# Setup phase: one weight group is turned while the group before it is mixed, with two sets of turned weights

## The chip, the cores and the metric

The kernel runs on one core of one Trainium2 chip. The metric is the device time of one launch in microseconds; three runs of the kernel before gave 2410.3 us as median (2406.4 to 2411.33).

TensorE (PE in the profile) multiplies and transposes into PSUM, ScalarE (ACT) and VectorE (DVE) read PSUM and write SBUF, GpSimd (POOL) works in SBUF only, SyncE (SP) issues the DMAs. The engines run their own instruction streams and meet at semaphores only.

## What is computed

The reference is a small network over 4 x 512 tokens of width 512: an attention with random features (L0), a layer that routes each token to one of 64 tiles and adds a spline of 8 of its dimensions, a differential attention (L1), and a gated feed-forward whose three weight matrices are turned by Walsh-Hadamard transforms. For this change two parts matter:

```
# L1 feed-forward: x and weights pass through a Hadamard transform (fwht) with signs SU
W_up, W_gate: 2048 x 512      W_down: 512 x 2048
# L0 feed-forward, routing of each token (xf: normalised tokens)
input_sigs = sign(xf)
best_cluster = argmax(input_sigs @ cluster_sigs.T)
tile_idx = argmax(where(in_cluster, input_sigs @ tile_sigs.T, -inf))
x_slice = xf at the 8 dimensions of that tile; tile_min, tile_max over all tokens of a tile
```

The kernel folds the transforms into the weights once, in a setup phase, and does the routing of the L0 layer for the first use of it in the same phase. Everything else comes after that phase.

## The kernel before

All weights are kept as two float16 parts, high and low: ScalarE writes the high part of a PSUM block, VectorE the difference between the block and its high part.

The setup phase (`setup_sync`, `setup_pool`, `setup_tensor`, `setup_scalar`, `setup_vector`) first turns three groups of L0 attention weights (`first`, lines 797 and 932 on), normalises the tokens, and then runs a loop of four chunks i. A chunk takes three weight groups: two of W_up or W_gate (g = 0, 1) and 128 rows of W_down (g = 2), and routes 512 tokens.

- `turned(i, g)` is four tiles r. TensorE transposes 4 blocks of 128x128 float32 into PSUM bank 0 or 1 (`turn_rows`, line 719), ScalarE writes the high part (line 810), VectorE the low part (line 951), into the one buffer pair `wt_hi`, `wt_lo`. Tile r waits for the low part of tile r-2, which frees its bank.
- `mixed(i, g)` is four blocks kc, and waits for all four tiles of the group. For g = 0, 1 a block is 8 matmuls of 512 columns (line 762), for g = 2 it is 2 (lines 765, 766); into bank 2 or 3, then high part (lines 817, 822) and low part (lines 959, 965). Block kc waits for the low part of block kc-2.
- The W_down rows are scaled by ScalarE (`scale_down`, line 827) and go through four butterfly stages on GpSimd (lines 696, 697) before they are turned.
- The routing of a chunk is a chain over three engines: ScalarE normalises four token tiles (line 845); for each of four feature blocks c TensorE turns it (`route_turn`, line 459) and ScalarE adds gamma and beta and takes the sign (lines 512, 515); TensorE scores the tiles (`route_key`, lines 470, 472), VectorE picks the best (lines 530, 531), TensorE and ScalarE turn the choice (`route_hot`, lines 481, 522), TensorE spreads it as a mask and VectorE multiplies it in (lines 492, 540), TensorE gathers the eight dimensions (`route_slice`, line 502), VectorE keeps the extremes (`route_ends`, lines 548 to 558).

Each engine has these steps in a fixed order written out in its setup function; TensorE's is turned 0, mixed 0, four route turns, turned 1, key, mixed 1, hot, turned 2, masks, two blocks of mixed 2, slice, the other two blocks. SyncE loads the weight groups in order into two halves of `nat`, and stores each finished W_down chunk (`store_down`) to DRAM.

After the loop `minmax_tensor` and `minmax_vector` (lines 597 to 607) reduce the extremes, and the next phase starts.

Of the kernel before, what the change touches and what calls it, by code (L numbers as in the profile page):

```python
# [28 lines left out]
NCH = NTOK // CH  # L29
# [248 lines left out]
def place(k, nc, ctx):  # L278
# [35 lines left out]
    k.wd_nat, a = v.at(a, [P, 4, INTER], F32)  # L314
# [4 lines left out]
    k.wt_hi, a = v.at(a, [P, KC, HID], F16)  # L319
    k.wt_lo, a = v.at(a, [P, KC, HID], F16)  # L320
# [309 lines left out]
def setup_sync(k, sp):  # L630
# [54 lines left out]
def setup_pool(k, e):  # L685
    s = k.s
    e.wait_ge(s["all_chain"], 5)
    for o in range(4):
        e.wait_ge(s["wd_scaled"], o + 1)
        bufs = [k.wd_nat[:, o, :], k.wd_tmp]  # L690
# [17 lines left out]
def tile_base(i, g):  # L708

    return 4 * (W0_GROUPS + 3 * i + g)  # L710


def setup_tensor(k, pe):
# [24 lines left out]
    def turned(i, g):  # L738
        tile = tile_base(i, g)
        if g < 2:  # L740
            buf = (W0_GROUPS + g) % 2
            pe.wait_ge(s[f"nat_in{buf}"], 32 * ((W0_GROUPS + g) // 2 + 1 + i))
        else:
            pe.wait_ge(s["wd_mixed"], i + 1)
        for r in range(4):
            pe.wait_ge(s["wt_lo"], tile + r - 1)
            if g < 2:
                native(buf, r, UP_BANK[r % 2])
            else:
                turn_rows(lambda c, r=r: k.wd_nat[:, i, (4 * r + c) * P:(4 * r + c + 1) * P], UP_BANK[r % 2])  # L750

    def mixed(i, g, blocks):
        pe.wait_ge(s["wt_lo"], tile_base(i, g) + 4)
        for kc in blocks:
            pe.wait_ge(s["had_lo"], 4 * (3 * i + g) + kc + 3)
            bank = HAD_BANK[kc % 2]
            if g < 2:
                n = 0
                for jc in range(KC):
                    sign = k.had16n if bin(kc & jc).count("1") & 1 else k.had16  # L760
                    for part in (k.wt_hi, k.wt_lo):
                        ins = pe.matmul(k.ps[:, bank, :], sign, part[:, jc, :], start=(n == 0), stop=(n == 7))  # L762
                        n += 1
            else:
                pe.matmul(k.ps[:, bank, :], k.had16, k.wdt_hi[:, 4 * kc:4 * kc + 4, :], start=True, stop=False)
                ins = pe.matmul(k.ps[:, bank, :], k.had16, k.wdt_lo[:, 4 * kc:4 * kc + 4, :], start=False, stop=True)
            ins.then_inc(s["had_done"], 1)

    pe.wait_ge(s["ss_chain"], 5)
    for i in range(NCH):  # L770
        turned(i, 0)
        mixed(i, 0, range(KC))
        for c in range(KC):
            route_turn_tensor(k, pe, i, 1, c, ROUTE_BANK)
        turned(i, 1)
        route_key_tensor(k, pe, i, 1, KEY_BANK)
        mixed(i, 1, range(KC))
        route_hot_tensor(k, pe, i, 1, ROUTE_BANK[0])
        turned(i, 2)
        for c in range(KC):  # L780
            route_mask_tensor(k, pe, i, 1, c, ROUTE_BANK)
        mixed(i, 2, (0, 1))
        route_slice_tensor(k, pe, i, 1, KEY_BANK)
        mixed(i, 2, (2, 3))
    pe.wait_ge(s["had_lo"], 4 + 4 * 3 * NCH)


def setup_scalar(k, e):
# [15 lines left out]
    def turned(i, g):  # L804
        tile = tile_base(i, g)
        for r in range(4):
            e.wait_ge(s["nat_turned"], tile + r + 1)
            src = k.ps[:, UP_BANK[r % 2], :].rearrange("p (c m) -> p c m", c=KC)
            dst = k.wt_hi[:, :, r * P:(r + 1) * P] if g < 2 else k.wdt_hi[:, 4 * r:4 * r + 4, :]
            e.activation(dst, src, ACT.Copy, scale=W_SCALE).then_inc(s["wt_hi"], 1)  # L810

    def mixed(i, g):
        for kc in range(KC):
            e.wait_ge(s["had_done"], 4 * (3 * i + g) + kc + 1)
            src = k.ps[:, HAD_BANK[kc % 2], :]
            if g < 2:
                e.activation(ug_block(k, 2 * i + g, 0, kc), src.rearrange("p (f m) -> p f m", m=P), ACT.Copy,
                             scale=k.su_ug[:, kc:kc + 1]).then_inc(s["had_hi"], 1)
            else:
                if kc == 0 and i:  # L820
                    e.wait_ge(s["wdo_out"], 32 * i)
                e.activation(k.wdo_hi[:, 4 * kc:4 * kc + 4, :], src.rearrange("p (c m) -> p c m", c=4), ACT.Copy,
                             scale=float(INTER) ** -0.5).then_inc(s["had_hi"], 1)

    def scale_down(o):
        e.wait_ge(s[f"wd_in{o}"], 16)
        e.activation(k.wd_nat[:, o, :], k.wd_nat[:, o, :], ACT.Copy, scale=k.wscale_dp[:, o:o + 1])\
            .then_inc(s["wd_scaled"], 1)
# [12 lines left out]
    for i in range(NCH):  # L841
        turned(i, 0)
        for u in range(TPC):
            t = i * TPC + u
            ins = e.activation(k.y[:, u, :], k.x[:, t, :], ACT.Identity, bias=k.wide[6][:, t:t + 1],
                               scale=k.wide[5][:, t:t + 1])
        ins.then_inc(s["z_scaled"], 1)
        mixed(i, 0)
        for c in range(KC):
            route_sign_scalar(k, e, i, 1, c, ROUTE_BANK)  # L850
        turned(i, 1)
        if i + 1 < NCH:
            scale_down(i + 1)
        mixed(i, 1)
        route_hot_scalar(k, e, i, 1, ROUTE_BANK[0])
        turned(i, 2)
        mixed(i, 2)
# [43 lines left out]
def setup_vector(k, V):  # L901
# [43 lines left out]
    def turned(i, g):  # L945
        for r in range(4):
            e.wait_ge(s["wt_hi"], tile_base(i, g) + r + 1)
            src = k.ps[:, UP_BANK[r % 2], :].rearrange("p (c m) -> p c m", c=KC)
            hi, lo = [w[:, :, r * P:(r + 1) * P] if g < 2 else x[:, 4 * r:4 * r + 4, :]
                      for w, x in ((k.wt_hi, k.wdt_hi), (k.wt_lo, k.wdt_lo))]  # L950
            e.scalar_tensor_tensor(out=lo, in0=src, scalar=W_SCALE, in1=hi, op0=ALU.mult, op1=ALU.subtract)\  # L951
                .then_inc(s["wt_lo"], 1)

    def mixed(i, g, blocks):
        for kc in blocks:
            e.wait_ge(s["had_hi"], 4 * (3 * i + g) + kc + 1)
            src = k.ps[:, HAD_BANK[kc % 2], :]
            if g < 2:
                e.scalar_tensor_tensor(out=ug_block(k, 2 * i + g, 1, kc), in0=src.rearrange("p (f m) -> p f m", m=P),
                                       scalar=k.su_ug[:, kc:kc + 1], in1=ug_block(k, 2 * i + g, 0, kc),  # L960
                                       op0=ALU.mult, op1=ALU.subtract).then_inc(s["had_lo"], 1)
            else:
                if kc == 0 and i:
                    e.wait_ge(s["wdo_out"], 32 * i)
                e.scalar_tensor_tensor(out=k.wdo_lo[:, 4 * kc:4 * kc + 4, :], in0=src.rearrange("p (c m) -> p c m", c=4),
                                       scalar=float(INTER) ** -0.5, in1=k.wdo_hi[:, 4 * kc:4 * kc + 4, :],
                                       op0=ALU.mult, op1=ALU.subtract).then_inc(s["had_lo"], 1)
                e.wait_ge(s["had_lo"], 4 + 4 * (3 * i + g) + kc + 1)
                e.sem_inc(s["wdo_lo"], 1)
# [7 lines left out]
    for i in range(NCH):  # L977
        turned(i, 0)
        mixed(i, 0, range(KC))
        turned(i, 1)  # L980
        route_choice_vector(k, V, i, 1, KEY_BANK)
        mixed(i, 1, range(KC))
        turned(i, 2)
        for c in range(KC):
            route_pick_vector(k, V, i, 1, c, ROUTE_BANK)
        mixed(i, 2, (0, 1))
        mixed(i, 2, (2, 3))
        route_ends_vector(k, V, i, 1, KEY_BANK)
# [1671 lines left out]
def bass_macaron(nc, d):  # L2660
    with ExitStack() as ctx:
# [7 lines left out]
        k.wdt_hi = k.wt_hi.rearrange("p c (b m) -> p (c b) m", m=P)  # L2669
        k.wdt_lo = k.wt_lo.rearrange("p c (b m) -> p (c b) m", m=P)  # L2670
# [158 lines left out]
```

## Time and profile before

| what | value |
|---|---|
| median of three runs | 2410.3 us |
| profiled execution: its own time, its span | 2407.47 us, 2405.7 us |
| PE, DVE, ACT, POOL busy over the span | 2087.0, 1228.1, 749.2, 221.2 us |
| setup loop with its last reduction | 38.3 to 254.4 us of the span |
| PE busy in it, granted clock | 166.09 of 216.10 us, 0.75 |
| DVE, ACT busy in it | 90.94 us, 97.82 us |

The span is the stretch between the first and the last instruction of the profiled execution. The granted clock is the share of TensorE's full clock that the chip allowed: 1.00 is 2.4 GHz and 0.50 is 1.2 GHz. A row of a timeline merges instructions of one kind that follow each other: start, duration, engine, line, operation, output and input, count, and in brackets the idle time before it with what ended it.

### The profile page before, as it was taken

How to read it: one execution, taken by the hardware profiler on the slowest of the kernel's cores; microseconds unless marked ns; L12 is line 12 of the kernel's file. 1: busy time of each engine (PE TensorE's matmuls, PEld its weight loads, DVE VectorE, ACT ScalarE, POOL GpSimd, SP SyncE). 2: the span in 40 equal slices, each digit the busy share in tenths (PEclk: the TensorE clock that was granted, in tenths of full speed). 3: DMA queues.
4: the chain of work that ended last, by engine and by line, in shares of the span. 5: the costliest groups of instructions: out<-in, count | busy, mean ns of one | idle time of the engine just before them, and what ended most of it. 6: DMA issues, size and time to landing. Idle time of an engine off the chain costs nothing. (4 is left out here: it accounts for less than half of the span.)

```text
span 2405.7 us, 29600 instructions
## 1 busy us (share of the span) xinstructions
PE 2087.0 (87%) x12078; PEld 996.0 (41%) x12078; DVE 1228.1 (51%) x2281; ACT 749.2 (31%) x1163; POOL 221.2 (9%) x164
## 2 busy tenths in 40 slices
PE   4777486878877479999999999989998999999998
PEld 3444333333435234444444444434443444444443
DVE  5444445657554445555557445653566356623332
ACT  4444123333242122223234322442235123511211
POOL 3341021211110000000100010001000000000000
PEclk7777577988785589999999999999999999999999
DMA  6211402021112212222111111111111111222322
GB/s 247 88 53 18 164 10 48 22 37 28 31 49 58 93 55 94 97 97 75 41 43 62 36 62 54 53 45 53 53 54 53 53 39 34 78 88 98 114 92 74
DMA packets 90978, 158.75 MB, mean 66 GB/s; under 512 B 44182, under 2 KB 55772, under 8 KB 86108
## 3 DMA queue, kind: packets, MB, share of 16 engines
q1 hardware_dynamic: 90844, 156.86, 20.3%
q8 instruction: 96, 1.57, 0.3%
q14 instruction: 38, 0.31, 0.0%
HBM read 128.52 MB, written 18.87 MB: 61 GB/s over the span
## 5 line engine op out<-in xcount | busy, mean ns | idle before, releaser
L1130 PE MATMUL ps<-arena 128*128 128x512 f16 (+1 forms) x4512 | 1019.1, 381 | 19.8 <-DVE arena L1893 12.9
L1130 PEld LDWEIGHTS ps<-arena 128*128 128x128 f16 x4512 | 437.2, 99 | 541.4 <-issue 48.5
L1838 PE MATMUL ps<-arena 128*128 128x512 f16 x1536 | 348.9, 383 | 29.5 <-DVE arena L1884 16.3
L1838 PEld LDWEIGHTS ps<-arena 128*128 128x128 f16 x1536 | 147.4, 98 | 207.3 <-issue 29.2
L1860 ACT ACTIVATE arena<-ps,arena 128x512 f32<-128x512 f32 x128 | 87.6, 684 | 362.3 <-PE ps L1130 362.0
L1893 DVE SCALAR_TENSOR_TENSOR arena<-arena,ps 128x512 f32<-128x512 f32 x128 | 87.9, 686 | 210.1 <-ACT arena L1860 209.5
L2447 ACT ACTIVATE arena<-ps 128x1024 f32<-128x1024 f32 (+3 forms) x128 | 90.1, 704 | 253.7 <-PE ps L2356 253.7
L2552 DVE CAST arena<-arena 128x1024 f16<-128x1024 f32 (+3 forms) x128 | 66.6, 520 | 149.7 <-ACT arena L2447 147.7
L2518 DVE TENSOR_REDUCE arena<-ps 128x2 f32<-128x256 f32 (+3 forms) x128 | 99.6, 819 | 65.1 <-PE ps L2300 65.1
L1902 DVE SCALAR_TENSOR_TENSOR arena<-ps,arena 128x512 f32<-128x512 f32 x128 | 95.8, 748 | 39.3 <-PE ps L1130 39.1
L1921 DVE SCALAR_TENSOR_TENSOR arena<-ps,arena 128x512 f32<-128x512 f32 x64 | 44.0, 687 | 139.6 <-PE ps L1838 139.4
L2554 DVE TENSOR_TENSOR arena<-arena 128x1024 f16<-128x1024 f32 (+3 forms) x128 | 111.4, 870 | 4.4
L1529 DVE TENSOR_TENSOR arena<-ps,arena 128x256 f32<-128x256 f32 x128 | 47.8, 418 | 100.9 <-PE ps L1214 100.9
L2498 POOL TENSOR_TENSOR arena<-arena 128x512 f16<-128x512 f32 x32 | 37.1, 1159 | 656.7 <-ACT arena L2425 656.7
L1884 DVE TENSOR_TENSOR arena<-arena 128x512 f16<-128x512 f32 x128 | 91.7, 716 | 4.0 <-ACT arena L1852 4.0
L1755 PE MATMUL ps<-arena 128*128 128x128 f32 x192 | 33.6, 335 | 67.0 <-ACT arena L1970 67.0
L1852 ACT ACTIVATE arena<-arena 128x512 f16<-128x512 f32 x128 | 79.7, 622 | 17.5 <-DVE arena L1902 17.5
L719 PE MATMUL ps<-arena 128*128 128x128 f32 x240 | 43.8, 341 | 43.0 <-DVE arena L951 30.2
L762 PE MATMUL ps<-arena 128*128 128x512 f16 x256 | 72.0, 451 | 5.7 <-DVE arena L951 5.7
L2354 PE MATMUL ps<-arena 32*128 32x512 f16 (+3 forms) x768 | 72.9, 293 | 0.0
L2502 POOL TENSOR_TENSOR arena<-arena 128x512 f32<-128x512 f32 x16 | 18.6, 1161 | 582.0 <-DVE arena L2565 582.0
L2422 ACT ACTIVATE arena<-ps 128x512 f32<-128x512 f32 x32 | 19.1, 597 | 166.7 <-PE ps L1130 166.7
(267 smaller groups left out, 2466.5 us busy)
## 6 DMA issues: line engine op xcount, KB each, us to landing
arena<-wug_dram SPq DMA_DIRECT2D x128, 512.0 KB, 3.3
arena<-wd_hi_dram SPq DMA_DIRECT2D x16, 1024.0 KB, 5.0
arena<-wd_lo_dram SPq DMA_DIRECT2D x16, 1024.0 KB, 7.3
arena<-arena SPq DMA_DIRECT2D x144, 64.0 KB, 2.1
wug_dram<-arena SPq DMA_DIRECT2D x4, 2048.0 KB, 16.5
arena<-_attn_hidden_states_dram SPq DMA_DIRECT2D x4, 1024.0 KB, 11.8
arena<-in_L_ffn_W_up_dram SPq DMA_DIRECT2D x8, 512.0 KB, 4.4
arena<-in_L_ffn_W_down_dram SPq DMA_DIRECT2D x4, 1024.0 KB, 8.0
```

The lines of the kernel that those rows point to most:

```text
L762: ins = pe.matmul(k.ps[:, bank, :], sign, part[:, jc, :], start=(n == 0), stop=(n == 7))
L1130: ins = pe.matmul(out, left[a](c), right[b](c), start=(at == 0), stop=(at == 3 * n - 1))
L1838: ins = pe.matmul(k.ps[:, bank, :], act[x][:, slot, cols], wd[y][:, f, :], start=(f == 0 and m == 0), stop=(f == 7 and m == 2))
L1852: e.activation(k.act_hi[:, g % ACT_SLOTS, :], k.prod[:, g % 2, :], ACT.Copy).then_inc(s["f_hi"], 1)
L1860: e.activation(k.th[:, g % 2, :], k.ps[:, GATE_BANK, :], ACT.Tanh, scale=k.wscale[:, FB + a:FB + a + 1])\
L1884: e.tensor_tensor(k.act_lo[:, g % ACT_SLOTS, :], k.prod[:, g % 2, :], k.act_hi[:, g % ACT_SLOTS, :], ALU.subtract)\
L1893: e.scalar_tensor_tensor(out=th, in0=th, scalar=1.0, in1=k.ps[:, GATE_BANK, :], op0=ALU.add, op1=ALU.mult)\
L1902: e.scalar_tensor_tensor(out=k.prod[:, g % 2, :], in0=k.ps[:, UP_HALF_BANK, :], scalar=k.wscale[:, a:a + 1], in1=th, op0=ALU.mult, op1=ALU ...
L2354: pe.matmul(k.ps[:, bank, queries], x[rows, 4 + b, keys], y[rows, b, queries], start=False, stop=False)
L2447: e.activation(k.p32[:, t % 2, :, queries], k.ps[:, 0:2, queries], ACT.Exp, scale=SCORE).then_inc(s["c_exp"], 1)
L2518: e.tensor_reduce(k.mx[:, u, 4 * b + 2 * j:4 * b + 2 * j + 2], k.ps[:, bank:bank + 2, 0:(u + 1) * P], AXX, ALU.max).then_inc(s["c_max"], 1)
L2554: e.tensor_tensor(k.p_lo[:, t % 2, :, queries], k.p32[:, t % 2, :, queries], k.p_hi[:, t % 2, :, queries], ALU.subtract).then_inc(s["c_p_l ...
```

## The change

The loop over chunks and groups becomes one loop over n = 0 to 12 (n = 3i + g) and over steps r = 0 to 3. Step (n, r) is tile r of group n and then block r of group n-1. The turned weights get a second buffer pair (side n % 2). To make room `wd_nat` keeps three rows of chunks instead of four; the fourth load of W_down goes into the first slot again, behind a wait on TensorE's transposes of group 2, and is issued one place later in SyncE's order. The routing is cut into its steps and each stands at a fixed place (`ROUTE_AT`: groups after 3i, step). `scale_down(i + 1)` moves from behind `turned(i, 1)` to behind the normalising of chunk i. All instructions on the four compute engines are the same in kind and number.

```diff
-    k.wd_nat, a = v.at(a, [P, 4, INTER], F32)
+    k.wd_nat, a = v.at(a, [P, 3, INTER], F32)
...
-    k.wt_hi, a = v.at(a, [P, KC, HID], F16)
-    k.wt_lo, a = v.at(a, [P, KC, HID], F16)
+    k.wt = []
+    for side in range(2):
+        hi, a = v.at(a, [P, KC, HID], F16)
+        lo, a = v.at(a, [P, KC, HID], F16)
+        k.wt.append((hi, lo))
...
-        if g < 4:
-            sp.dma_start(k.wd_nat[:, g, :], d["L1_ffn_W_down"][g * P:(g + 1) * P, :]).then_inc(s[f"wd_in{g}"], 16)
+        o = g if g < 3 else 3
+        if g < 3 or g == 4:
+            if o == 3:
+                sp.wait_ge(s["nat_turned"], 4 * (W0_GROUPS + 3))
+            sp.dma_start(k.wd_nat[:, o % 3, :], d["L1_ffn_W_down"][o * P:(o + 1) * P, :]).then_inc(s[f"wd_in{o}"], 16)
...
+ROUTE_AT = {"stats": (0, 1), "turn": ((0, 3), (1, 0), (1, 1), (1, 2)), "sign": ((1, 0), (1, 1), (1, 2), (1, 3)),
+            "key": (2, 0), "hot": (2, 1), "mask": ((2, 2), (2, 2), (2, 3), (2, 3)), "slice": (3, 0), "ends": (3, 1)}
...
+def route_now(n, r, what, c=None):
+    at = ROUTE_AT[what] if c is None else ROUTE_AT[what][c]
+    i = n // 3 if at[0] < 3 else n // 3 - 1
+    return i if 0 <= i < NCH and (n - 3 * i, r) == at else None
...
# setup_tensor
+    def turned(n, r):
...
+        pe.wait_ge(s["wt_lo"], tile_base(n) + r - 1)
...
+    def mixed(n, kc):
+        if kc == 0:
+            pe.wait_ge(s["wt_lo"], tile_base(n) + 4)
+        pe.wait_ge(s["had_lo"], 4 * n + kc + 3)
...
-    for i in range(NCH):
-        turned(i, 0)
-        mixed(i, 0, range(KC))
-        for c in range(KC):
-            route_turn_tensor(k, pe, i, 1, c, ROUTE_BANK)
-        turned(i, 1)
-        route_key_tensor(k, pe, i, 1, KEY_BANK)
-        mixed(i, 1, range(KC))
-        route_hot_tensor(k, pe, i, 1, ROUTE_BANK[0])
-        turned(i, 2)
-        for c in range(KC):
-            route_mask_tensor(k, pe, i, 1, c, ROUTE_BANK)
-        mixed(i, 2, (0, 1))
-        route_slice_tensor(k, pe, i, 1, KEY_BANK)
-        mixed(i, 2, (2, 3))
+    for n in range(GROUPS + 1):
         for r in range(4):
+            if n < GROUPS:
+                turned(n, r)
+            if n:
+                mixed(n - 1, r)
+            for c in range(KC):
+                i = route_now(n, r, "turn", c)
+                if i is not None:
+                    route_turn_tensor(k, pe, i, 1, c, ROUTE_BANK)
...
# setup_scalar: per step turned, mixed, then
+            i = route_now(n, r, "stats")
+            if i is not None:
+                for t in range(i * TPC, (i + 1) * TPC):
+                    ins = e.activation(k.y[:, t % TPC, :], k.x[:, t, :], ACT.Identity, bias=k.wide[6][:, t:t + 1],
+                                       scale=k.wide[5][:, t:t + 1])
+                ins.then_inc(s["z_scaled"], 1)
+                if i + 1 < NCH:
+                    scale_down(i + 1)
...
# then route_sign and route_hot; setup_vector: per step turned, mixed, then choice, picks, ends
```

## Rows read from the trace of the kernel before

**Rows 1.** The page: the granted clock in 40 slices of the span.

```profile
PEclk7777577988785589999999999999999999999999
```

**Rows 2.** Busy time by stretch: stretch, length, then PE, PEld, DVE, ACT, POOL, clock, DMA.

```profile
140.80:195.20 54.40, 42.55 (x197) 25.08 (x196) 22.77 (x38) 24.98 (x38) 18.62 (x8) 0.75 0.19 59
38.30:254.40 216.10, 166.09 (x776) 97.67 (x776) 90.94 (x152) 97.82 (x152) 74.56 (x32) 0.75 0.19 56
```

**Rows 3.** Groups of instructions, 38 to 254 us: busy and mean, idle before.

```profile
L762 PE MATMUL ps<-arena 128*128 128x512 f16 x256 | 72.0, 451 | 5.7 <-DVE arena L951 5.7
L719 PE MATMUL ps<-arena 128*128 128x128 f32 x184 | 32.2, 325 | 30.2 <-DVE arena L951 30.2
...
L817 ACT ACTIVATE arena<-ps,arena 128x512 f16<-128x512 f32 x32 | 22.0, 687 | 46.5 <-PE ps L762 46.5
```

**Rows 4.** Timeline of PE, from the first chunk's slice into the second chunk.

```profile
78.16 6.92 PE L502 MATMUL ps<-arena 128*128 128x8 f32 x32
...
86.58 1.87 PE L719 MATMUL ps<-arena 128*128 128x128 f32 x8
91.98 1.97 PE L719 MATMUL ps<-arena 128*128 128x128 f32 x8 [3.53 <-DVE arena L951]
95.37 8.63 PE L762 MATMUL ps<-arena 128*128 128x512 f16 x32 [1.41 <-DVE arena L951]
...
107.27 1.04 PE L719 MATMUL ps<-arena 128*128 128x128 f32 x8
...
112.77 0.23 PE L470 MATMUL ps<-arena 1*128 1x64 f16 x1
...
114.60 5.57 PE L762 MATMUL ps<-arena 128*128 128x512 f16 x15
```

**Rows 5.** Busy time and granted clock of the later part of that mixing.

```profile
98.80:103.80 5.00, 5.00 (x25) 2.11 (x23) 2.25 (x3) 2.06 (x3) 0.00 (x0) 1.00 0.00 1
```

**Rows 6.** Timeline of ACT.

```profile
36.37 2.00 ACT L827 ACTIVATE arena<-arena 128x2048 f32<-128x2048 f32 x1 [3.43 <-DVE arena L898]
...
94.48 2.92 ACT L845 ACTIVATE arena<-arena 128x512 f32<-128x512 f32 x4
...
106.76 0.63 ACT L515 ACTIVATE arena<-arena 128x512 f16<-128x512 f32 x1
107.30 0.76 ACT L512 ACTIVATE arena<-ps,arena 128x512 f32<-128x512 f32 x1
...
109.96 1.06 ACT L810 ACTIVATE arena<-ps 128x512 f16<-128x512 f32 x2
```

**Rows 7.** Timeline of DVE.

```profile
88.30 0.30 DVE L548 TENSOR_SCALAR arena<-arena 128x256 f32<-128x256 f16 x1
...
91.24 1.29 DVE L951 SCALAR_TENSOR_TENSOR arena<-ps,arena 128x512 f16<-128x512 f32 x2
...
103.03 0.75 DVE L959 SCALAR_TENSOR_TENSOR arena<-ps,arena 128x512 f16<-128x512 f32 x1 [0.99 <-ACT arena L817]
...
128.84 1.28 DVE L540 TENSOR_TENSOR arena<-ps,arena 128x512 f32<-128x512 f32 x2
```

**Rows 8.** Busy time and granted clock of three other stretches.

```profile
12.00:18.00 6.00, 5.92 (x33) 5.68 (x32) 4.42 (x11) 3.76 (x7) 0.00 (x0) 1.00 1.05 393
...
130.80:140.80 10.00, 10.00 (x41) 8.07 (x41) 2.16 (x4) 1.79 (x3) 3.56 (x2) 0.50 0.00 0
...
143.00:144.00 1.00, 0.00 (x0) 0.00 (x0) 0.93 (x4) 0.35 (x1) 0.00 (x0) 1.00 0.28 72
```

**Rows 9.** Timeline of POOL: the last butterfly of the first chunk.

```profile
55.05 2.37 POOL L697 TENSOR_TENSOR arena<-arena 128x1024 f32<-128x1024 f32 x1
```

**Rows 10.** Timeline around the loop's end.

```profile
251.88 1.26 SPq L664 DMA_DIRECT2D wd_lo_dram<-arena  x1
...
254.00 0.29 DVE L558 TENSOR_TENSOR arena<-arena 128x128 f32<-128x128 f32 x1
...
260.70 0.55 DVE L2767 COPY arena<-arena 24x768 f32<-24x768 f32 x1 [4.51 <-DMA arena<-in_L_attn_bo_dram]
```

More of the change, by code:

```diff
@@ L736, in setup_tensor @@
             native(g % 2, r, r)
-    def turned(i, g):
-        tile = tile_base(i, g)
+    def turned(n, r):
+        i, g = n // 3, n % 3
+        if r == 0:
+            if g < 2:
+                group = W0_GROUPS + 2 * i + g
+                pe.wait_ge(s[f"nat_in{group % 2}"], 32 * (group // 2 + 1))
+            else:
+                pe.wait_ge(s["wd_mixed"], i + 1)
+        pe.wait_ge(s["wt_lo"], tile_base(n) + r - 1)
         if g < 2:
-            buf = (W0_GROUPS + g) % 2
-            pe.wait_ge(s[f"nat_in{buf}"], 32 * ((W0_GROUPS + g) // 2 + 1 + i))
-        else:
-            pe.wait_ge(s["wd_mixed"], i + 1)
-        for r in range(4):
[L746 to L767, printed above, removed]
@@ L785, in setup_tensor @@
-    pe.wait_ge(s["had_lo"], 4 + 4 * 3 * NCH)
+            native((W0_GROUPS + g) % 2, r, UP_BANK[r % 2])
+        else:
+            turn_rows(lambda c: k.wd_nat[:, i % 3, (4 * r + c) * P:(4 * r + c + 1) * P], UP_BANK[r % 2])
+    def mixed(n, kc):
+        if kc == 0:
+            pe.wait_ge(s["wt_lo"], tile_base(n) + 4)
+        pe.wait_ge(s["had_lo"], 4 * n + kc + 3)
+        out = k.ps[:, HAD_BANK[kc % 2], :]
+        if n % 3 < 2:
+            m = 0
+            for jc in range(KC):
+                sign = k.had16n if bin(kc & jc).count("1") & 1 else k.had16
+                for part in range(2):
+                    ins = pe.matmul(out, sign, k.wt[n % 2][part][:, jc, :], start=(m == 0), stop=(m == 7))
+                    m += 1
+        else:
+            for part in range(2):
+                ins = pe.matmul(out, k.had16, k.wdt[n % 2][part][:, 4 * kc:4 * kc + 4, :], start=(part == 0),
+                                stop=(part == 1))
+        ins.then_inc(s["had_done"], 1)
@@ new lines, in setup_tensor @@
+    pe.wait_ge(s["ss_chain"], 5)
+    for n in range(GROUPS + 1):
+        for r in range(4):
+            if n < GROUPS:
[6 more added lines that the diff above has]
+                    route_turn_tensor(k, pe, i, 1, c, ROUTE_BANK)
+            i = route_now(n, r, "key")
+            if i is not None:
+                route_key_tensor(k, pe, i, 1, KEY_BANK)
+            i = route_now(n, r, "hot")
+            if i is not None:
+                route_hot_tensor(k, pe, i, 1, ROUTE_BANK[0])
+            for c in range(KC):
+                i = route_now(n, r, "mask", c)
+                if i is not None:
+                    route_mask_tensor(k, pe, i, 1, c, ROUTE_BANK)
+            i = route_now(n, r, "slice")
+            if i is not None:
+                route_slice_tensor(k, pe, i, 1, KEY_BANK)
@@ L788, in setup_scalar @@
+    pe.wait_ge(s["had_lo"], 4 + 4 * GROUPS)
 def setup_scalar(k, e):
@@ L840, in setup_scalar @@
     scale_down(0)
[L841 to L857, printed above, removed]
+    for n in range(GROUPS + 1):
+        for r in range(4):
+            if n < GROUPS:
+                turned(n, r)
+            if n:
+                mixed(n - 1, r)
+            i = route_now(n, r, "stats")
+            if i is not None:
+                for t in range(i * TPC, (i + 1) * TPC):
[4 more added lines that the diff above has]
+                    scale_down(i + 1)
+            for c in range(KC):
+                i = route_now(n, r, "sign", c)
+                if i is not None:
+                    route_sign_scalar(k, e, i, 1, c, ROUTE_BANK)
+            i = route_now(n, r, "hot")
+            if i is not None:
+                route_hot_scalar(k, e, i, 1, ROUTE_BANK[0])
 def setup_stats_vector(k, V):
@@ L943, in first @@
                 .then_inc(s["wt_lo"], 1)
[L945 to L969, printed above, removed]
+    def turned(n, r):
+        e.wait_ge(s["wt_hi"], tile_base(n) + r + 1)
+        e.scalar_tensor_tensor(out=turned_block(k, n, r, 1),
+                               in0=k.ps[:, UP_BANK[r % 2], :].rearrange("p (c m) -> p c m", c=KC), scalar=W_SCALE,
+                               in1=turned_block(k, n, r, 0), op0=ALU.mult, op1=ALU.subtract).then_inc(s["wt_lo"], 1)
@@ L976, in setup_vector @@
     setup_norm_vector(k, V)
[L977 to L988, printed above, removed]
+    for n in range(GROUPS + 1):
+        for r in range(4):
+            if n < GROUPS:
+                turned(n, r)
+            if n:
+                mixed(n - 1, r)
+            i = route_now(n, r, "key")
+            if i is not None:
+                route_choice_vector(k, V, i, 1, KEY_BANK)
+            for c in range(KC):
+                i = route_now(n, r, "mask", c)
+                if i is not None:
+                    route_pick_vector(k, V, i, 1, c, ROUTE_BANK)
+            i = route_now(n, r, "ends")
+            if i is not None:
+                route_ends_vector(k, V, i, 1, KEY_BANK)
 def apply_tensor(k, pe, i, n):
```

67 lines of the change are left out of this document (41 added, 26 removed).

## The prediction

> **What bounds the kernel now.** The page comes first: the granted clock stands at 0.7 to 0.8 in four of the first five slices and is low in the next ones too, against 0.9 later [rows 1]; the change touches only the setup loop, which lies in the first slices. So next the busy time by stretch. From 38.3 to 254.4 us PE is busy 166.09 of 216.10 us, ACT 97.82, DVE 90.94, at a clock of 0.75; a chunk takes 54.40 us with PE busy 42.55 [rows 2]. Two things are wrong in the loop: 50 us in which PE waits, and matmuls at half clock. The groups of instructions name the wait: transposes sit idle 30.2 us until VectorE has written a low part (L951), the first matmul of a mixing another 5.7 us, and neither waits for a DMA [rows 3]. The timeline of one chunk shows how [rows 4]: eight transposes at 86.58, idle, eight more at 91.98, idle, and the mixing at 95.37: 8.8 us for 3.8 us of work, and PE has nothing else in its order to do. Of the mixing, 32 matmuls in 8.63 us, the first 3.4 us are slow; from 98.8 on the clock stands at 1.00 [rows 5]. So a block of eight matmuls costs 3.4 us at 1.2 GHz and (8.63 - 3.4) / 3 = 1.74 us at 2.4 GHz.
>
> What follows the loop is released by its end (the last extremes, then a bias load issued after them) [rows 10], so what the loop saves comes off the span nearly one for one.
>
> **The change, part by part.** Durations used. A tile of four transposes costs PE 0.43 us at full clock and 0.9 at half (eight in 1.04, with the pipeline's tail, and in 1.87) [rows 4]; a W_down block a quarter of a wide one. ACT: 0.53 for a tile (two in 1.06), 0.76 + 0.63 for a sign step, 2.92 for normalising, 2.00 for scaling W_down [rows 6], 0.69 for a block [rows 3]. DVE: 0.65 a tile (two in 1.29), 0.75 a block, 0.64 a pick (two in 1.28), 2.9 for the extremes (88.30 to the next group at 91.24) [rows 7].
>
> *Two sets of turned weights, tile and block in turn.* This removes the wait at the start of a mixing and fills the idle time between tiles with blocks. The waits are the old ones in new places. Tile r waits for the low part of tile r-2, and behind it in PE's queue stand the block of the same step and the route step; two steps are at least 4.3 us of PE work in the wide groups, and the hand-over PE to ACT to DVE and back costs about 2.5 us (a tile's 0.9 at half clock, ACT 0.6, DVE 0.7 and the gaps), so it is met there. A block waits for the block two before; from PE's end to DVE's end is 0.25 + 0.72 + 0.75 = 1.7 us (gap, ACT, DVE), and a block and two tiles lie between. Now a chunk, laid out by all three engines, in three parts.
>
> Part A, from the last block of group 3i-1 (time 0) to the first block of group 3i. DVE has the low part of that block and two picks behind it: 1.7 + 1.3 = 3.0 us, so the slice starts at 3.2. The slice (L502) took 6.92 us [rows 4], and the slices here run at half clock (0.50 in the stretch that holds the second one) [rows 8]. At full clock it has no row. From above it is bounded by 6.9 us; from below by half, 3.4, as transposes with weights of the same shape halve. It would start with the clock up and lose it on the way: I take 5.1 us, the middle, and keep both ends. Then PE does tile 1 and block 1, ACT evicts them (2.1 us after the slice), and now ACT is the queue: normalising and scaling stand ahead of tile 2, 2.92 + 2.00, until 7.1 us; tiles 2 and 3 and the block between them take it to 8.9, DVE to 9.9. The first block of group 3i starts 10.0 us after the slice. Part A is 3.2 + 5.1 + 10.0 = 18.3 us. The scaling comes here from a place where ACT had time: 2.0 us of these are a cost of the move.
>
> Part B, the four blocks of group 3i beside the tiles of 3i+1 and the sign steps. The first block runs at half clock after PE idled in part A: 3.4 us. The other three steps are bounded by ACT, 0.53 + 0.69 + 0.76 + 0.63 = 2.6 us and a gap, 2.75 each (PE has 0.43 + 1.74 + 0.43 = 2.6): 8.2 us. Then 1.4 us until the fourth tile, evicted behind the third sign step, is there. 13.0 us.
>
> Part C, the blocks of group 3i+1: PE sets the pace, as ACT (1.2 us) and DVE (1.4 us, 2.7 with picks) have little more per step. Block 1.7, key 1.9 (112.77 to 114.60, at half clock) [rows 4], three steps of 0.43 + 1.74 = 6.5, hot and two masks 0.8 (estimated by their columns). 10.9 us.
>
> A chunk is 18.3 + 13.0 + 10.9 = 42.2 us instead of 54.4.
>
> *Start.* In group 0 ACT has scaling (until 38.3), two tiles, normalising, scaling again, two tiles: 38.3 + 1.06 + 2.92 + 2.00 + 1.06 = 45.4, DVE 46.2, first block at 46.4. Group 2 is turned from about 58 us on, and POOL ends the W_down rows it needs at 57.4 [rows 9]: just in time. Parts B and C end at 46.4 + 13.0 + 10.9 = 70.3.
>
> *End.* Three more chunks: 70.3 + 126.6 = 196.9. Then 3.2 for the picks, 5.1 for the slice, 5.2 for block 1 through ACT and DVE (2.3) and the extremes (2.9): 210.4, where the trace has 254.3 (254.00 + 0.29) [rows 10]: 43.9 us less.
>
> *Tail.* VectorE now has two blocks behind the extremes, 1.5 us, and SyncE stores the last W_down chunk behind them (the second half alone took 1.26 us to issue) before it may load the biases; now the wait from the extremes to the end of that load is 6.4 us (254.3 to 260.70) [rows 10]. I charge 4 us, between 1.5 (the blocks alone) and 6 (the load lands late behind the store).
>
> *At no cost.* The fourth W_down load goes into a slot free since group 2 and is needed three groups (some 40 us) later. Loads of the next groups are issued when a half of `nat` is turned and needed two groups later; the waits of stores stand ahead of some of them in SyncE's order, with more than a group to spare. If that cover were gone, PE rows would wait for a DMA.
>
> Sum: 43.9 - 4 = 40 us. The profiled execution took 2407.47 us around a span of 2405.7, 2.8 us below the median; against the median the forecast is 2410.3 - 40 = 2370 us.
>
> **The clock, weighed.** That parts B and C run at full clock is what the forecast needs. The rows for it: PE is at 0.50 up to 140.8, and after two small blocks and eight transposes that follow the slice it stands at 1.00 at 143 us, with PE already idle again [rows 8]. A step of part B has 1.74 us of wide matmuls in 2.75, more than that.
>
> The Trainium skill ("TensorE: Matmul & The Clock Gate", Part 4, PE-mode transpose) says that transposes do not count as busy for the clock gate the way matmuls do. By it, a loop that mixes transposes into matmuls dilutes the work that counts, which speaks for the first rival below. The trace half agrees: from 12 to 18 us PE did 32 transposes and nothing else and stayed at 1.00 [rows 8].
>
> **Rivals.**
> 1. *The alternation keeps the clock at 1.2 GHz* (slower). 28 blocks that I put at 1.74 us would take 3.4, 47 us, and tiles and route steps some 15 us more: 40 - 62 = -22, 2432 us. It turns the sign from about 24 slow blocks of 28. For it: no stretch of this trace thins out matmuls in this way. Against it: the rows just named. 4%.
> 2. *The waits only move.* Each engine serves two streams in one order, so a late eviction holds both. If each of seven steps of B and C in four chunks pays half a hand-over again, 1.2 us, 34 us are lost: 2404 us. For it: ACT is nearly full in part B. Against it: every wait reaches two steps back. 12%, for a gain between 5 and 20 us.
> 3. *More than forecast.* Slice at full clock (4 x 1.7 = 7 us), and the clock back before part B's first block (4 x 1.7 = 7 us): 54 us, 2356 us. 16%.
> 4. *SyncE's order holds a load, or POOL is late*: the wait appears on a DMA or on L697 and eats the gain, 2405 to 2415 us. 3%.
>
> The forecast's own case has 65%.
>
> **How the numbers follow.** Ends: 7 us each way for the slice, 7 each way for when the clock rises, 2 for the tail, and up to 0.3 us for hand-overs left out in each of 52 steps, 15 us, one way only. Best 2354, worst 2401; I give 2352 to 2395, which leaves out rivals 1 and 4 and part of 2. A change under 0.2% (5 us) could not be told from none. Faster by more holds the forecast, rival 3 and most of 2: 0.92; same 0.03; slower 0.05.
>
> **What would show it.** The idle time ahead of L719 and L762 (36 us together) falls to about 15, nearly all of it in part A. The granted clock of the loop rises from 0.75 to 0.85 or more. After each slice PE idles while ACT runs L845 and L827. The last row of the extremes moves from 254.0 to about 210, and what follows keeps its length but for 4 us. It would be wrong if L762's blocks stay 3.4 us long, if ACT idles ahead of L512 in part B, or if PE waits for a DMA or for POOL.

## The result and the profile after

The kernel after takes 2364.3 us as median of four runs (2363.24 to 2367.23), the kernel before, in the same comparison, 2410.2 (2406.4 to 2411.33): a ratio of 0.9817, interval 0.9801 to 0.9832. Forecast were 2370 us, 40 us less; 45.9 us came off. The profiled execution took 2363.24 us around a span of 2361.5, 44.2 us less than the span before. (The 1.7 us between 45.9 and 44.2 are scatter: the profiled execution before lies 2.7 us under its median, the one after 1.0 us under its own.)

The granted clock of the page, the busy time of the loop (columns as in [rows 2]), and the groups of PE instructions in it (as [rows 3]; L790 was L762, L747 was L719, L505 was L502):

```profile
PEclk7886769797966599999999999999999999999999
```
```profile
38.30:205.80 167.50, 144.53 (x776) 90.16 (x776) 89.05 (x150) 95.67 (x152) 74.67 (x32) 0.83 0.24 72
```
```profile
L790 PE MATMUL ps<-arena 128*128 128x512 f16 x256 | 65.6, 402 | 2.8 <-DVE arena L985 2.8
L747 PE MATMUL ps<-arena 128*128 128x128 f32 x184 | 33.7, 315 | 11.5 <-DVE arena L985 11.5
L505 PE MATMUL ps<-arena 128*128 128x8 f32 x128 | 23.2, 323 | 5.3 <-DVE arena L543 5.3
```

The loop with its last extremes takes 167.5 us instead of 216.1 [rows 2]. The wait ahead of transposes and wide blocks is 14.3 us (11.5 + 2.8) instead of 35.9 [rows 3], the clock 0.83 instead of 0.75. PE's busy time falls by 21.6 us (166.09 to 144.53) with the same instructions, and its idle time by 27.0 (50.0 to 23.0): the two add up to the loop's gain. VectorE's count falls by two because its last two blocks now stand behind the extremes. Nothing in the loop waits for a DMA or for the butterflies.

PE from the first slice to the second chunk's blocks (beside [rows 4]):

```profile
72.87 5.24 PE L505 MATMUL ps<-arena 128*128 128x8 f32 x32 [1.21 <-DVE arena L543]
...
77.96 1.09 PE L747 MATMUL ps<-arena 128*128 128x128 f32 x4
78.85 1.06 PE L794 MATMUL ps<-arena 128*128 128x512 f16 x2
...
83.41 0.66 PE L462 MATMUL ps<-arena 128*128 128x128 f32 x4 [0.84 <-ACT arena L884]
86.67 1.09 PE L747 MATMUL ps<-arena 128*128 128x128 f32 x4 [2.61 <-DVE arena L985]
88.02 3.60 PE L790 MATMUL ps<-arena 128*128 128x512 f16 x8 [0.26 <-DVE arena L985]
91.41 0.85 PE L462 MATMUL ps<-arena 128*128 128x128 f32 x4
92.09 0.60 PE L747 MATMUL ps<-arena 128*128 128x128 f32 x4
92.53 1.89 PE L790 MATMUL ps<-arena 128*128 128x512 f16 x8
...
95.13 1.89 PE L790 MATMUL ps<-arena 128*128 128x512 f16 x8
```

Read the durations of equal blocks: 3.60 us at 88.02 and 1.89 at 92.53 (each with the tail that the model adds to a duration), and from 92.53 on one block starts every 2.60 us. And ACT in the same stretch, which is why PE idles 2.61 us: normalising (L884) and scaling (L861) stand ahead of the eviction of the tile (L843).

```profile
80.44 2.92 ACT L884 ACTIVATE arena<-arena 128x512 f32<-128x512 f32 x4
83.26 1.99 ACT L861 ACTIVATE arena<-arena 128x2048 f32<-128x2048 f32 x1
85.15 0.58 ACT L843 ACTIVATE arena<-ps 128x512 f16<-128x512 f32 x1
```

The loop's end, DVE and then SyncE's queue, which stores W_down (L667) and then loads the biases (L687, L688) (beside [rows 10]):

```profile
205.54 0.29 DVE L561 TENSOR_TENSOR arena<-arena 128x128 f32<-128x128 f32 x1
...
216.72 0.55 DVE L2805 COPY arena<-arena 24x768 f32<-24x768 f32 x1 [7.56 <-DMA arena<-in_L_attn_bo_dram]
```
```profile
208.04 1.24 SPq L667 DMA_DIRECT2D wd_lo_dram<-arena  x1
209.32 2.99 SPq L687 DMA_DIRECT2D arena<-in_L_attn_bv_dram  x1
212.36 0.58 SPq L688 DMA_DIRECT2D arena<-in_L_attn_bo_dram  x1
```

The extremes end 48.5 us earlier (205.83 against 254.29), and the copy behind them starts 10.9 us later than that, instead of 6.4: 4.5 us are given back. At the copy 44.0 of the span's 44.2 us are in.

### The profile page after: what moved, and what is told of

It reads as the page before. It is cut to its first block and busy times, and to the rows that moved or that the text cites. A ratio compares the mean times of both kernels' runs of the same rounds, so it can differ in the third digit from the quotient of the medians.

```text
span 2361.5 us, 29596 instructions
## 1 busy us (share of the span) xinstructions
PE 2062.1 (87%) x12078; PEld 987.3 (42%) x12078; DVE 1227.2 (52%) x2281; ACT 746.9 (32%) x1163; POOL 220.9 (9%) x164
## 5 line engine op out<-in xcount | busy, mean ns | idle before, releaser
L1169 PEld LDWEIGHTS ps<-arena 128*128 128x128 f16 x4512 | 436.4, 99 | 542.8 <-issue 48.5
L1877 PE MATMUL ps<-arena 128*128 128x512 f16 x1536 | 349.0, 383 | 29.5 <-DVE arena L1923 16.3
L790 PE MATMUL ps<-arena 128*128 128x512 f16 x256 | 65.6, 402 | 2.8 <-DVE arena L985 2.8
L747 PE MATMUL ps<-arena 128*128 128x128 f32 x240 | 45.3, 334 | 24.3 <-DVE arena L985 11.5
```

Source lines behind the costliest of these rows:

```text
L1169: ins = pe.matmul(out, left[a](c), right[b](c), start=(at == 0), stop=(at == 3 * n - 1))
L1877: ins = pe.matmul(k.ps[:, bank, :], act[x][:, slot, cols], wd[y][:, f, :], start=(f == 0 and m == 0), stop=(f == 7 and m == 2))
```

## The experiments

Times are medians; "gain" is the difference to the kernel before in the same comparison, whose median was 2406.5 us for the first four kernels, 2408.0 for the next four and 2409.3 for the last four (three comparisons, each on another chip). The last three columns come from one profiled execution each: where the last row of the extremes starts, where the copy behind the loop starts, and how much of the span is left from there.

| kernel | us | gain | ratio, interval | last extremes start | copy starts | span left |
|---|---|---|---|---|---|---|
| the kernel before | | | | 254.00 | 260.70 | 2145.0 |
| the change | 2364.3 | 45.9 | 0.9817 (0.9801 to 0.9832) | 205.54 | 216.72 | 2144.8 |
| the change again | 2362.9 | 43.6 | 0.9824 (0.9808 to 0.9840) | 205.80 | 217.81 | 2143.2 |
| e1_whole_groups | 2375.2 | 31.2 | 0.9862 (0.9838 to 0.9885) | 213.00 | 224.24 | 2148.6 |
| e2_routing_lumps | 2363.7 | 42.8 | 0.9818 (0.9802 to 0.9835) | 205.79 | 217.13 | 2146.4 |
| e7_short_slice | 2341.7 | 64.8 | 0.9733 (0.9717 to 0.9749) | 185.28 | 196.39 | 2140.5 |
| e3_scale_late | 2371.3 | 36.7 | 0.9850 (0.9837 to 0.9864) | 214.06 | 225.41 | 2143.1 |
| e4_slice_late | 2351.7 | 56.2 | 0.9768 (0.9755 to 0.9782) | 190.45 | 201.45 | 2145.1 |
| e5_bias_apart | 2354.5 | 53.5 | 0.9784 (0.9771 to 0.9798) | 204.94 | 208.59 | 2139.4 |
| e8_warm | 2355.7 | 52.3 | 0.9777 (0.9764 to 0.9791) | 199.93 | 211.68 | 2144.6 |
| e9_late_apart | 2342.0 | 67.3 | 0.9714 (0.9699 to 0.9729) | 190.51 | 194.16 | 2145.5 |
| e10_late_apart_warm | 2334.9 | 74.4 | 0.9688 (0.9675 to 0.9701) | 191.82 | 195.47 | 2145.3 |
| e11_scale_ahead | 2360.9 | 48.4 | 0.9789 (0.9775 to 0.9804) | 201.56 | 213.23 | 2149.1 |
| e12_all | 2332.0 | 77.3 | 0.9682 (0.9667 to 0.9697) | 183.80 | 187.45 | 2140.1 |

Only the bias wait of four kernels (e5, e9, e10, e12) was changed behind the copy, and yet the span left varies from 2139.4 to 2149.1 us. So a difference of a few us between two medians is laid to the loop only where the loop's end in the traces moves by as much.

**The change again** gives the scale for what a repeat moves.

> The changed kernel once more, on the same chip as the three that follow, to compare them with. Every theory: 2363 to 2367 us, the last row of the extremes at about 206 us of the span.

2362.9 us, 0.1 us under the range, and the same loop's end to 0.3 us. Within the loop the repeat isn't the same: the last chunk's first wide block takes 3.23 us, where the change had 1.90, and the last slice 5.38 instead of 6.66.

**Two sets, but whole groups.** All four tiles, then all four blocks, in all three instruction streams; the routing and the scaling keep the places that the change gave them:

```diff
         for r in range(4):
             if n < GROUPS:
                 turned(n, r)
+        for r in range(4):
             if n:
                 mixed(n - 1, r)
```

> The second set of turned weights stays, the alternation goes: on every engine the four tiles of group n come together, then the four blocks of group n-1. Theory (tile and block in turn fill the waits): tiles 2 and 3 of each group wait again for the low parts of tiles 0 and 1, which stand behind the last block and sign step on ScalarE; about 1.2 us in parts with a free ScalarE, 3.5 us beside the signs, about 25 to 30 us in all 13 groups: 2388 to 2396 us, most of it as idle time ahead of the transposes. Rival (the second set alone brings the gain, since the mixing no longer waits for its own tiles): 2364 to 2370 us.

```profile
L790 PE MATMUL ps<-arena 128*128 128x512 f16 x256 | 65.5, 401 | 0.0
L747 PE MATMUL ps<-arena 128*128 128x128 f32 x184 | 32.4, 323 | 23.4 <-DVE arena L987 23.4
L505 PE MATMUL ps<-arena 128*128 128x8 f32 x128 | 15.7, 263 | 1.4 <-DVE arena L543 1.4
```

It fell between the two. By the medians everything but the alternation is worth 31 of the 43 to 46 us, and the alternation adds 12. The traces make the second share smaller: at the copy this kernel is 36.5 us ahead of the kernel before and 6.4 behind the change again, and the other 5.4 us between the two profiled executions arise behind the copy, where the kernels are the same. With a group turned ahead the blocks never wait (0.0); without the alternation transposes wait 23.4 us instead of 11.5, and part of that comes back at the slices, three of which start without idle time and take 3.63 us each (15.7 us for four instead of 23.2). What the second set does without the routing's and the scaling's new places no run shows.

**Routing in lumps.** All feature turns, signs and masks of a chunk at one place each:

```diff
-"turn": ((0, 3), (1, 0), (1, 1), (1, 2)), "sign": ((1, 0), (1, 1), (1, 2), (1, 3)),
+"turn": ((1, 0),) * 4, "sign": ((1, 0),) * 4,
-"mask": ((2, 2), (2, 2), (2, 3), (2, 3))
+"mask": ((2, 2),) * 4
```

> The alternation stays, the routing is taken in lumps: all four feature turns and signs after block 0 of part B, all four masks and picks at step 2 of part C. Theory (TensorE's order blocks behind a chain that goes to and fro): about 2 us per chunk at the signs, since ScalarE is the limit there anyway, and 3 us at the masks: 20 us over four chunks, 2380 to 2388 us. Rival (where the routing stands does not matter, only that blocks and tiles alternate): 2364 to 2368 us.

The theory fell, the rival's number held: the same time. But the trace shows a trade, and not the absence of effect that the rival named:

```profile
L747 PE MATMUL ps<-arena 128*128 128x128 f32 x184 | 32.1, 304 | 20.0 <-DVE arena L985 19.6
L505 PE MATMUL ps<-arena 128*128 128x8 f32 x128 | 14.5, 253 | 0.0
```

Transposes wait 8.5 us more and the mask products 7.6 us where they had waited for nothing, but the picks are through long before the slice, which waits for nothing (5.3 us less) and runs at full clock throughout: 14.5 us for four instead of 23.2. So the stepwise routing as such is worth nothing here; what it gains in the steps it loses at the slice.

**A quarter of the slice.** In the setup phase each slice does 4 of its 16 products, which the trace shows as 8 of 32 matmuls (so the eight dimensions are incomplete):

```diff
         for c in range(KC):
+            if one and c:
+                continue
```

> Leaves out 12 of the 16 matmuls of each slice in the setup loop, so the extremes are taken over a part of the features only. Theory (the slice lies whole on the path, and while it runs the granted clock falls, which makes the next wide block slow): the slice falls from 5.1 to 6.7 us to about 1.3, 4 x 4.3 = 17 us, and up to 3 x 1.7 = 5 us more where the clock then stays up: 2342 to 2348 us. Rival (part A is bounded by ScalarE's queue and VectorE's extremes, the slice is half covered): 2352 to 2358 us.

The time is the theory's within 0.3 us, 21 us against the change again, but only its first half is borne out. The four slices take 4.5 us instead of 23.2, 18.7 us less, and the loop ends 20.3 us earlier than in the change: the slice lies on the path with its whole length. The blocks behind it are no faster on the whole: the first blocks of the three chunks take 2.86, 3.44 and 3.03 us, where the change had 3.60, 3.50 and 1.90.

**The scaling moved behind the one-hot of the same chunk**, out of the stretch behind the slice:

```diff
                 ins.then_inc(s["z_scaled"], 1)
-                if i + 1 < NCH:
-                    scale_down(i + 1)
...
                 route_hot_scalar(k, e, i, 1, ROUTE_BANK[0])
+                if i + 1 < NCH:
+                    scale_down(i + 1)
```

> The scaling of the next W_down rows moves from behind the normalising in part A to behind the choice in part C, where ScalarE has time. Theory (its 2.0 us stand in the queue ahead of tile 2 and so ahead of the next wide block; where the extremes run too, VectorE is free 1.5 us earlier only): 2.0 + 3 x 1.5 = 5 to 6 us less than the changed kernel, 2357 to 2359 us. Rival (part A is bounded by VectorE's extremes or by GpSimd, which now gets its rows later): no gain, 2363 us or more.

It got slower than the change, by 7 to 9 us. The rival's "2363 us or more" covers the time, but it spoke of a missing gain; neither named a loss. DVE's extremes, and POOL's butterflies at the same time, which the scaling releases:

```profile
79.92 1.16 DVE L551 TENSOR_SCALAR arena<-arena 128x256 f32<-128x256 f16 x1
81.00 0.18 DVE L554 TENSOR_REDUCE arena<-ps 128x4 f32<-128x32 f32 x1
...
81.42 1.97 DVE L557 TENSOR_SCALAR arena<-arena 128x4 f32<-128x4 f32 x1
83.42 2.79 DVE L559 TENSOR_TENSOR arena<-arena 128x512 f32<-128x512 f32 x1
86.24 1.02 DVE L560 TENSOR_REDUCE arena<-arena 128x128 f32<-128x512 f32 x1
```
```profile
78.57 2.36 POOL L703 TENSOR_TENSOR arena<-arena 128x1024 f32<-128x1024 f32 x1
81.01 2.35 POOL L702 TENSOR_TENSOR arena<-arena 128x1024 f32<-128x1024 f32 x1
83.32 2.34 POOL L703 TENSOR_TENSOR arena<-arena 128x1024 f32<-128x1024 f32 x1
```

In the change L551, L557 and L559 take 0.29, 0.16 and 0.69 us. Here the first two end when POOL's instruction does, at 81.08 against 80.93 and 83.39 against 83.36; the third ends at 86.21, POOL's end at 85.66 and 0.55 more. The operations beside them that read PSUM keep their 0.18 us. The extremes start 1.5 us earlier and end 3.2 us later (87.59 against 84.35), and behind them wait the low parts: PE idles 5.89 us ahead of the tile instead of 2.61. In the next two chunks it idles 3.95 and 4.31 us instead of 2.61 and 0.94; together that is 8.0 us more, and the loop ends 8.5 later. In the change POOL begins its butterflies at 85.39, 1.0 us after the extremes, and misses them.

The Trainium skill has this ("SBUF — State Buffer", Who interferes with whom): VectorE and GpSimd share a port pair as an exclusive lock, held for a whole instruction; a VectorE instruction with two SBUF inputs, or in a two-port mode, takes part, and one with at most one SBUF input outside these modes does not. This trace agrees for L559, which has two SBUF inputs, and for the operations that read PSUM. L551 and L557 have one and were held too, to within 0.15 us of POOL's end; by the page they would have to be in a two-port mode, which no run here shows. I had not weighed this beforehand.

**The slice a step later**, behind block 1 instead of ahead of it; ACT waits for it before it overwrites the tokens:

```diff
-"slice": (3, 0)
+"slice": (3, 1)
...
+                if i:
+                    e.wait_ge(s["r_slice"], i)
```

> The slice stands one step later, behind tile 1 and block 1, and the normalising waits for the slice itself. Theory (TensorE idles 1.2 us ahead of the slice, tile 1 and block 1 fit there, and after the slice ScalarE starts the normalising at once): 2.6 us per chunk on three chunks and 2.3 us at the end, 10 us less than the changed kernel, 2352 to 2356 us. Rival (the slice's end is not what ScalarE's queue starts from; or the clock is lost as before and tile and block only change places): at most 3 us, 2360 us or more.

```profile
71.83 3.74 PE L505 MATMUL ps<-arena 128*128 128x8 f32 x32 [0.34 <-DVE arena L543]
```

The sum is as the theory had it (0.3 us under its range), the parts are not. Tile 1 and block 1 fill the wait for the picks, and ACT starts the normalising when the slice ends; but three of four slices also keep the clock and take 3.74 us, which the theory had not priced. Of the 15.1 us by which the loop ends earlier than in the change, the slices are 5.8, and 1.0 is there ahead of the first slice already (by the medians the gain is 10 to 13 us; the profiled execution is the fastest of its five). The last slice took 6.19, with 0.59 us of idle time ahead of it.

**The bias loads on another semaphore**, waited for only where the biases are used (TensorE's wait falls to 128 too):

```diff
-    sp.dma_start(k.bv, ...).then_inc(s["b_in"], 16)
-    sp.dma_start(k.bo, ...).then_inc(s["b_in"], 16)
+    sp.dma_start(k.bv, ...).then_inc(s["const_in"], 16)
+    sp.dma_start(k.bo, ...).then_inc(s["const_in"], 16)
...
-        dve.wait_ge(s["b_in"], 160)
+        dve.wait_ge(s["b_in"], 128)
...
+            dve.wait_ge(s["const_in"], 48)
```

> The two bias loads at the loop's end count on a semaphore of their own, which VectorE waits for only 27 us later, where they are long there; nothing else changes. Theory (VectorE's wait of 7.6 us for the last bias load is on the path, 4.5 us of the alternation's gain were lost in that tail): 7 us less than the changed kernel, 2355 to 2358 us. Rival (the next phase waits for other loads or for the store of W_down anyway): within 2 us of the changed kernel, 2361 to 2365 us.

```profile
204.94 0.29 DVE L561 TENSOR_TENSOR arena<-arena 128x128 f32<-128x128 f32 x1
...
208.59 0.55 DVE L2805 COPY arena<-arena 24x768 f32<-24x768 f32 x1
```

As the theory had it, and half a us more: the loop is as in the change (its end 0.6 us earlier), the copy waits for nothing and starts 8.1 us earlier.

**Added products** in an unused bank around the first feature turn of chunks 1 to 3:

```diff
+                    if c == 0 and i:
+                        warm(4)
                     route_turn_tensor(k, pe, i, 1, c, ROUTE_BANK)
+                    if c == 0 and i:
+                        warm(8)
```

> Adds 12 matmuls of 512 columns per chunk into an unused bank, 4 ahead of the first feature turn and 8 behind it, where TensorE idles in part A. Theory (the wide blocks at the start of part B run at half clock because TensorE idled before them): first blocks of 1.7 instead of 3.4 us in two or three chunks, 3 to 5 us less, 2358 to 2361 us. Rival (the clock falls during the slice and comes back by the blocks alone, or the added matmuls run at half clock and delay the next tile): 0 to 5 us more, 2363 to 2369 us.

```profile
83.02 1.89 PE L800 MATMUL ps<-arena 128*128 128x512 f16 x8
85.80 0.63 PE L747 MATMUL ps<-arena 128*128 128x128 f32 x4 [0.88 <-DVE arena L993]
87.14 1.90 PE L790 MATMUL ps<-arena 128*128 128x512 f16 x8 [0.72 <-DVE arena L993]
```

By the medians it is more than expected, 6 to 9 us. In the trace the extremes end 5.6 us earlier than in the change, and 1.3 of these are there at the first slice, ahead of any added product; the other 4.3 lie in the theory's 3 to 5. Filling the idle time brings the first block of part B to 1.90 us in all three chunks (3.60, 3.50 and 1.90 in the change), and in chunk 1 the tile ahead of it to 0.63 where it took 1.09.

**Combinations, and the scaling once more.** e9 is e4 and e5, e10 adds the products of e8.

> The slice one step later (as e4_slice_late) together with the two bias loads on a semaphore of their own (as e5_bias_apart). Alone they gave 11.2 and 8.5 us against the changed kernel. Theory: they lie in different stretches (the loop, and the copy behind it), and add up, 19.7 us: 2341 to 2345 us. Rival: the wait behind the loop also covers something else that e4 moved earlier, and the sum falls short by over 4 us: 2347 or more.

> e9_late_apart with the 12 added 512-column products per chunk of e8_warm (4 ahead of the first feature turn, 8 behind it; their results are read by nobody). In e4's order TensorE still idles 1.2 us ahead of that turn and 2.6 behind it, and the first blocks behind it take 3.59 us against 1.89. Theory: three such blocks and the products about them come back to the full clock, 5 to 8 us less than e9: 2334 to 2339 us. Rival: the idle time is now shorter, the clock falls elsewhere anyhow, and the added products only cost their own time: 2342 to 2347 us.

e9: 2342.0 us, the two add up. e10: 2334.9, inside its theory by the medians, but the intervals of the ratios overlap and the profiled execution, the slowest of its five at 2342.57 us, ends the loop 1.3 us after e9's: its first three slices lost the clock (5.29, 4.93, 4.24 us) where e9's took 3.74. The first of them stands ahead of any added product, so the products are not what cost it the clock. Whether the products pay on top of e9 stays open.

In e11 the scalings for chunks 2 and 3 come a chunk ahead, and GpSimd waits until the extremes are done:

```diff
-                if i + 1 < NCH:
-                    scale_down(i + 1)
+                if i == 0:
+                    scale_down(1)
...
                 route_hot_scalar(k, e, i, 1, ROUTE_BANK[0])
+                if i + 2 < NCH:
+                    scale_down(i + 2)
...
         e.wait_ge(s["wd_scaled"], o + 1)
+        if o > 1:
+            e.wait_ge(s["routed"], o - 1)
```

> Against e3_scale_late, where the scaling of the W_down rows left the stretch behind the slice but GpSimd's butterflies then ran beside VectorE's extremes: here the scalings for chunks 2 and 3 are issued a chunk ahead, behind the one-hot of chunks 0 and 1, and GpSimd waits with them until the extremes of the routing one before are done, so that it works when it does in the changed kernel. Theory (contention was what made e3 slow, and a scaling costs what ScalarE holds TensorE up): ScalarE reaches the tile 2.0 us earlier, VectorE's extremes hold its second half until 84.35, so 1.3 to 2.0 us each for two scalings: 2359 to 2361 us, the operations of the extremes at their 0.29, 0.16 and 0.69 us. Rival (moving the scaling into the stretch of the feature turns is what costs, whoever is beside it): 2366 to 2372 us as e3.

```profile
80.46 0.16 DVE L557 TENSOR_SCALAR arena<-arena 128x4 f32<-128x4 f32 x1
80.65 0.69 DVE L559 TENSOR_TENSOR arena<-arena 128x512 f32<-128x512 f32 x1
```
```profile
82.93 2.35 POOL L704 TENSOR_TENSOR arena<-arena 128x1024 f32<-128x1024 f32 x1 [6.23 <-DVE arena L561]
```

As the theory had it, and it settles e3: with POOL behind the extremes these keep their lengths, and the loop ends 4.0 us earlier than in the change. By the medians it is 2 to 5 us faster than the change, about what can be told apart. A scaling costs part A 1.5 us: from the end of the slice to the first block it is 8.6 us in all three chunks here, against 10.06 in the change's two chunks with a scaling (VectorE's extremes hide the rest of its 2.0). So 2.9 of the 4.0 us are the two scalings, and what made e3 slow was the neighbour that its scaling released.

> e10_late_apart_warm with the scaling moved as in e11_scale_ahead. Theory: in this order the extremes are through before the tile, so the two scalings give their whole 2.0 us each, 4 us less than e10: 2330 to 2335 us. Rival: the stretch is then set by the normalising and the slice alone and GpSimd's later start is late for the W_down tiles: within 1 us of e10 or above it.

e12, all of it: 2332.0 us, the fastest, 77 us below the kernel before where the change is 44 to 46 below it. Its loop ends 8 us before e10's in the profiled executions; the medians, 2.9 us apart, don't separate the two.

## Why the prediction was right

*Part B and the clock.* First wide block of chunk 0: forecast 46.4, measured 46.42. First block at half clock 3.4, then full clock: 88.02 to 91.41 is 3.39. Forecast steps of 2.75 us measured 2.60 (92.53, 95.13, 97.73), and part B 12.3 us instead of 13.0. The bound was named wrongly: PE and not ACT sets the pace in these steps, for PE has no idle time in them, and ACT idles 0.30 us for it ahead of its block at 94.45; as the two differ by little, this cost the number nothing. Rivals 1 and 2 are out: every wide block behind the first of a chunk runs at full clock, and ACT never idles ahead of a sign step (L515: 0.0 us of idle). (Rival 1 was priced a little wrong: at its own 62 us for 28 blocks with what stands beside them, the sign turns at 18 slow blocks and not at 24. And the transposes at 1.00 in [rows 8], which the prediction has half agree, speak against it as far as they go.) In chunk 3 the first block too was at full clock (1.90 us at 169.67), one of the four that rival 3 priced at 7 us together; it was luck, for the repeat has 3.23 there. The clock over the loop is 0.83, where 0.85 or more was named as the sign.

*The slice.* Taken at 5.1 us between 3.4 and 6.9, measured 5.24, 5.53, 5.81 and 6.66, 2.8 us more for the four than the sum has. That the middle of two bounds came so near was luck. "It would start with the clock up and lose it on the way" is what the clock shows: 1.00 in the stretch ahead of it, 0.68 in the one that holds it.

```profile
69.00:73.00 4.00, 2.79 (x15) 1.14 (x13) 3.69 (x7) 1.79 (x4) 3.92 (x3) 1.00 0.02 4
73.00:78.00 5.00, 5.00 (x33) 5.00 (x33) 1.01 (x2) 0.00 (x0) 3.54 (x2) 0.68 0.00 0
```

At full clock throughout a slice takes 3.63 us, in all four of e2, with nothing idle ahead of them; the bound of 3.4 was near.

*Part A.* From the end of the slice to the first block 10.0 forecast, 10.06 measured (77.96 to 88.02), with the cause named: ACT's 2.92 + 1.99 us. Of the "2.0 us of these are a cost of the move" 1.5 us show in the trace (10.06 with a scaling, 8.60 in the chunk without); I had named no other place, and the first one I tried was worse (e3). Of PE's 14.3 us of idle time ahead of tiles and blocks some 8 lie in part A and 5.4 in the loop's first group, so "nearly all of it in part A" holds only with that group counted in.

*Part C.* Key 1.9 us forecast, from rows at half clock; it took 1.34 (102.18 to 103.52) with the clock up. Part C as a whole measured 11.0 all the same (100.34 to 111.32), as its three steps of tile and block took 6.9 us and not 6.5. A chunk was forecast at 42.2 and measured 41.3, 41.3 and 38.5 from slice to slice; the last is shorter as it has no scaling in part A, which the layout had left in (8.6 us from slice to block instead of 10.1), and its first block runs at full clock (1.6 less). So the loop's end, forecast at 210.4, came 4.6 us sooner: 0.6 until the first slice (73.5 forecast, 72.87 measured), 5.6 in the three chunks, and 1.6 lost again behind the last slice's start, as that slice took 6.66 us and not 5.1.

*Tail.* Forecast 4, measured 4.5, by the mechanism named: the copy waits 7.56 us for the bias load, which SyncE issues behind a store that waits for DVE's last block. The 4 us were a choice between 1.5 and 6. e5 shows that the whole of the wait is avoidable.

*Sum.* 48.5 - 4.5 = 44.0 at the copy against 43.9 - 4 = 39.9. The mechanism was right; the largest part of the 4 us is the last chunk, 3.7 us shorter than laid out.

What the prediction didn't say is which half of the change does it. "Removes the wait at the start of a mixing and fills the idle time between tiles" are two things: the first, with the overlap of groups that it brings and the new places of routing and scaling, is worth 31 us by the medians and 36.5 at the copy (e1), the second 12 and 6.4. And it gave the stepwise routing no price of its own; e2 makes it zero, net.

## What to carry to other kernels

In a loop over two stages with one buffer between them, price the second buffer and the alternation apart: here the kernel with the buffer and without the alternation already had most of the gain. Where TensorE idles for another engine, a gap can be paid twice, as idle time and as half clock in what comes behind it (e8): look for the small serial step that follows (here the slice) and put independent work ahead of it. Before a step is moved, look at what it releases: its successor moves with it, and may meet an engine that it used to miss. And before a few microseconds between two medians are laid to a cause, look in the traces where they arise.

## What the hardware showed

GpSimd's float32 `tensor_tensor` (2.35 us for 128x1024) held up VectorE's `tensor_scalar` and `tensor_tensor` from SBUF to SBUF until its own end, however small (e3): 0.16 us became 1.97, 1.90 and 1.90, 0.29 became 1.16, 1.39 and 1.74, 0.69 became 2.79; reductions and copies from PSUM in the same stretch kept 0.17 to 0.19 us. GpSimd's own instructions stayed at 2.34 to 2.41 us.

The slice, 32 matmuls of 128x8 in float32, took 3.63 us with the clock up throughout and 6.92 [rows 4] at half clock. Which it got follows the idle time that the rows show ahead of it, where the clock was up before. Without idle time it kept the clock in 9 of 9 whole slices (three of e1, four of e2, two of e12; 3.63 or 3.74 us). With 0.97 us or more it lost the clock within itself in all of them (in the change 4 of 4, in the repeat 4 of 4, 5.24 to 6.66 us). With 0.34 us it kept it in three slices of e4 and three of e9 and lost it in three of e10 and one of e12 (4.24 to 5.29 us), and with 0.59 us it took 6.18 to 6.28 us in e4, e9 and e10 and 3.88 in e12. What decides between these I can't tell from the runs.
